# Graph network on one core: seven lookup units in the second tile, twelve in the fourth, masks between evictions

## The reference

```
adj_d = adjacency with own nodes, some neighbours dropped by rank
vals  = where(adj_d > 0, x[neighbour, channel], inf)
s     = sort(vals, over neighbours)
agg   = sum over tau in (0.25, 0.5, 0.75) of w[tau] *
        (s[lo] + frac * (s[hi] - s[lo]))      # per node and channel
out   = relu((x + agg) @ W1 + b1) @ W2 + b2
```

## Time and profile before

| | us |
|---|---|
| median of 3 runs | 3977.04 (3974.77 to 3978.62) |
| profiled execution | 3979.06 |
| its span, first to last instruction | 3976.9 |
| DVE busy | 3539.2 |
| PE busy | 2607.1 |
| ACT busy | 1764.2 |

### The profile page before, as it was taken

How to read it: one execution, slowest core, us unless ns; L and a number is a source line. 1 busy time by engine, 2 the same in 40 slices (tenths; PEclk the granted TensorE clock), 3 DMA queues, 4 the chain that set the end, 5 groups by cost and what they waited for, 6 DMA issues and landing times. The chain is left out here.

```text
span 3976.9 us, 44051 instructions
## 1 busy us (share of the span) xinstructions
PE 2607.1 (66%) x14922; PEld 1083.3 (27%) x14922; DVE 3539.2 (89%) x6052; ACT 1764.2 (44%) x2295; POOL 56.6 (1%) x47
## 2 busy tenths in 40 slices
PE   0000042868686777777777878687868686877897
PEld 0000021223222232323222322232323222223665
DVE  7999989999989999899999998999998999964676
ACT  2112341646464545455554545463636364643232
POOL 0005000000000000000000000000000000000000
PEclk6555565979797989888988888898989898978777
DMA  1010000323232323232323222232323231322011
GB/s 24 0 32 11 0 6 18 44 41 65 35 56 36 59 32 58 32 58 34 56 35 54 38 50 41 46 46 43 49 40 50 38 66 28 54 46 41 33 42 32
DMA packets 242541, 156.06 MB, mean 39 GB/s; under 512 B 126472, under 2 KB 227994, under 8 KB 242330
## 3 DMA queue, kind: packets, MB, share of 16 engines
q1 hardware_dynamic: 238202, 152.36, 22.2%
q10 hardware_dynamic: 4128, 1.05, 0.2%
HBM read 39.07 MB, written 13.63 MB: 13 GB/s over the span
## 5 line engine op out<-in xcount | busy, mean ns | idle before, releaser
L901 ACT ACTIVATE hot<-bcast,eq_bias 128x1024 bf16<-128x1024 f32 x744 | 826.7, 1111 | 575.1 <-PE bcast L559 574.0
L1216 DVE SCALAR_TENSOR_TENSOR prod<-near,iota_b,rows 128x512 f32<-128x512 bf16 x768 | 571.9, 745 | 209.3 <-PE rows L571 107.1
L571 PE MATMUL rows<-hot,table 128*64 128x512 bf16 x4608 | 699.3, 411 | 68.0 <-DVE prod L1216 62.1
L547 PE MATMUL ring<-member,neigh_t 128*128 128x512 bf16 x2048 | 571.2, 419 | 183.2 <-ACT words L875 72.4
L558 PE MATMUL bcast<-idx_t,sel_a 128*128 128x512 f16 x744 | 304.5, 409 | 207.4 <-ACT hot L901 195.3
L580 PE MATMUL found_bank<-prod,sum_to 128*64 128x512 f32 x1536 | 432.6, 628 | 4.4 <-DVE prod L1216 4.4
L1276 DVE TENSOR_TENSOR picked<-picked 128x6144 uint16<-128x6144 uint16 (+2 forms) x192 | 387.5, 2018 | 0.7
L571 PEld LDWEIGHTS rows<-hot,table 128*64 128x64 bf16 x4608 | 222.0, 113 | 512.2 <-issue 401.6
L547 PEld LDWEIGHTS ring<-member,neigh_t 128*128 128x128 bf16 x2048 | 183.7, 105 | 599.6 <-issue 238.8
L474 PE MATMUL ring<-ident,swapped 128*128 128x128 f32 x32 | 6.2, 355 | 504.1 <-DVEq L1072 503.9
L559 PE MATMUL bcast<-idx_t,sel_a 128*128 128x512 f16 x744 | 303.6, 408 | 0.0
(11 more groups left out here) (325 smaller groups left out, 4245.6 us busy)
## 6 DMA issues: line engine op xcount, KB each, us to landing
near<-idx_bt SPq DMA_DIRECT2D x768, 128.0 KB
late<-in_adj_dram SPq DMA_DIRECT2D x16, 1024.0 KB, 5.3
adjt_d<-late SPq DMA_DIRECT2D x16, 512.0 KB, 2.7
adj_l<-adjt_d SPq DMA_DIRECT2D x16, 512.0 KB, 5.8
adj_s<-adjt_d SPq DMA_DIRECT2D x16, 512.0 KB, 3.6
parts_d<-parts SPq DMA_DIRECT2D x6, 512.0 KB, 5.1
table<-parts_d SPq DMA_DIRECT2D x192, 16.0 KB, 2.2
out_dram<-x_all SPq DMA_DIRECT2D x4, 512.0 KB, 3.8
```

The source lines that it names most:

```text
L547: ins = mm(ring[u % 2][:, :], kept_t[:, j, P * i:P * i + P], member[:, j, n // 2, 512 * (n % 2):512 * (n % 2) + 512], start=(j == 0), stop ...
L571: ins = mm(rows[u % 2][C * h:C * h + C, :], table[:, s, 2 * g8 + h, :], hot[:, u % HOT, h, :], start=(s == 0), stop=(s == 2))
L901: run(hot[:, u % HOT].rearrange(flat), spread_bank(l, u)[0][:, 0:2, :].rearrange(flat), ACT.Relu, bias=eq_bias[:, :]).then_inc(S["hot_read ...
L1216: stt(out=prod[:, u % DEEP, :], in0=near[:, u % NEAR, :], scalar=iota_b[:, :], in1=rows[u % 2][:, :], op0=ALU.is_equal, op1=ALU.mult).then ...
```

## The change

`PLACES` gives tile 1 seven units instead of nine (none behind its steps 1 and 2) and tile 3 twelve instead of ten (two behind step 4 and two behind step 6). `LEAD` goes from 0, 4, 13, 23, 33 to 0, 4, 11, 21, 33. PE and ACT used to work out how far ahead they run from the number of units of the tile; now a list `AHEAD` says it, and a `min` keeps them from running into the units of the tile behind too early. On ACT the masks of tile 1 stand one ahead of the eviction of chunk (1,6), one behind it, and one behind chunk (1,7). The copy to `x_now` moves from the middle of tile 0 to the end of `select`.

```diff
-PLACES = ((6, 7, 8, 9), (1, 2, 3, 4, 5, 6, 7, 8, 9), tuple(range(10)), tuple(range(10)))
+PLACES = ((6, 7, 8, 9), (3, 4, 5, 6, 7, 8, 9), tuple(range(10)), (0, 1, 2, 3, 4, 4, 5, 6, 6, 7, 8, 9))
+AHEAD = (0, -1, 1, 3)
@@ PE, select @@
-                        units(l, LEAD[i] + s + len(PLACES[i]) - 9)
+                        units(l, min(LEAD[i] + AHEAD[i] + s, LEAD[i + 1]))
@@ ACT, select @@
                 units(l, 4)
-                if l is not None:
-                    run(x_now[:, :, :], xb(l), ACT.Copy).then_inc(S["x_copied"], 1)
                 chunk(b, 1, 4)
                 units(l, 5)
                 chunk(b, 1, 5)
                 units(l, 6)
-                for k in range(TAUS):
-                    mask(b, 1, k)
+                mask(b, 1, 0)
                 chunk(b, 1, 6)
+                mask(b, 1, 1)
                 chunk(b, 1, 7)
+                mask(b, 1, 2)
                 for i in range(1, NT):
-                    level = LEAD[i] + len(PLACES[i]) - 9 + 2
+                    level = LEAD[i] + AHEAD[i] + 2
                     for s in range(10):
                         if i + 1 < NT:
                             if s == 2:
                                 mask(b, i + 1, 0)
-                                units(l, level + 2)
+                                units(l, min(level + 2, LEAD[i + 1] + 2))
                                 mask(b, i + 1, 1)
-                                units(l, level + 3)
+                                units(l, min(level + 3, LEAD[i + 1] + 2))
                                 mask(b, i + 1, 2)
                             if s < CW:
                                 chunk(b, i + 1, s)
-                        units(l, level + s)
+                        units(l, min(level + s, LEAD[i + 1] + 2))
+                if l is not None:
+                    run(x_now[:, :, :], xb(l), ACT.Copy).then_inc(S["x_copied"], 1)
```

## The result

The changed kernel takes 3919.99 us (median of 4 runs, 3918.85 to 3921.05) against 3976.95 us (4 runs, 3974.77 to 3978.62): a ratio of 0.9857, 95% interval 0.984 to 0.9874, that is 57 us or 1.4% faster. The forecast was 3908 with a range of 3885 to 3945.

What follows compares the result with a forecast made beforehand. DVE sets the pace, so only its idle time can be won: three tiles fall from 81.5 us by 4.8 a round, 67 us over 14 rounds plus 3 for round 1, together 70, giving 3908 us, range 3885 to 3945.

Steps and rivals of the forecast that it cites:

- The bound: DVE, busy 89% of the span, sets the pace; two rows of lookup waits hold 187.6 us; busy time stays near 3539.
- Tile 1: Second tile of a round: falls from 30.2 to 23.7 us, no wait before its first unit, 0.75 at its third.
- Tile 2: Third tile of a round: its wait stays and grows 0.3 us, so 27.2 us for 26.85.
- the one on the clock: PE's slow clock in five rounds of tile 1 goes with the shorter stand; if it stays, 8 us come back (3916).
- Tile 3: Last tile, two more units: 25.8 us for 24.5 with no wait; at most 3.3 us of waits a round.
- rival C: Tile 3, with twelve units, becomes PE's: at 2.6 us a unit 31.2 us, kernel 3988; loop expected about 2.0; chance 0.05.
- The last part of the round: The stretch behind the tiles: no term in the sum, so length as before.
- signs of being wrong: Tile 1 keeps over 2 us of waits, tile 3 gets over 1, or the round's last part gets longer.
- A: Tile 1's stall moves instead of going: DVE stands 3.5 us at unit 6, gain 1.8 a round, 3953; chance 0.14.
- B: PE gets ahead in tile 2 too, its 2.35 us of wait go: 3885 for half, 3861 for all; chance 0.08.
- D: No effect: the moved units cost in tile 3 what tile 1 gains, a loop near 2.5, 3977; chance 0.04.
- The queue of SP: SP's hold in tile 3 ends 0.66 us later, but unit 33 comes 1.3 later too: costs nothing.

Runs made afterwards that it cites:

- experiment 1: Kernel before, with only tile 1's masks placed one by one around the evictions of chunks (1,6) and (1,7): 3955.59 us, ratio 0.9949.
- experiment 2: Changed kernel with tile 1's three masks in a row again, ahead of both evictions, so the moved units without the mask change: 3935.50 us, ratio 0.9907.
- Experiment 6: Changed kernel plus eight matmuls whose output nothing reads, on PE just ahead of chunk (3,4) in tile 2: 3917.35 us, ratio 0.9847.
- Experiment 5: Kernel of experiment 4 with four more units moved from tile 2 (six left) to tile 3 (sixteen): 3923.76 us, ratio 0.9862.
- Experiment 7: Kernel of experiment 4 with PE issuing unit 39 ahead of the second count and the dense product in the last part: 3844.85 us, ratio 0.9662.
- experiment 3: Changed kernel with the copy to `x_now` put back in the middle of tile 0: 3917.92 us, ratio 0.9854.
- experiment 4: Changed kernel with ACT evicting chunk (i+1,2) behind the second mask instead of the third in tiles 1 and 2: 3873.39 us, ratio 0.9745.

## Why the prediction was right, and where it was off

**The bound.** The two rows of DVE's waits fell by 54.9 us of the 60.2 that the span lost. DVE's busy time, which I had forecast unchanged, fell from 3539.2 to 3533.4, though it runs the same 6052 instructions; no run says why.

**Tile 1.** Forecast 23.7 with no wait before its first unit and 0.75 before its third; measured 23.72 with 0.74 in seven of the thirteen rounds, 23.35 in one, and 22.88 with none in five. In the round at 1439.7, one of the five, PE starts chunk (2,0) 0.6 us ahead of DVE's tile, in the one at 2190.8 it is 0.3 behind it; I had worked out only the second kind. The average is 23.37, a gain of 6.9 where I had 6.5. The steps behind it held too: PE's stand before chunk (2,0) is 0.69 for the forecast 0.7; ACT evicts (2,2) 8.93 us into the tile (2222.10) for the forecast 9.05, and PE's chunk (2,4) follows 0.64 later for 0.6. Experiments 1 and 2 show that each part of the change gives a share of the gain.

**Tile 2.** Forecast 27.2, measured 27.15 in nine rounds. The step that failed is the one on the clock. I took the slow rounds as gone with the 2.66 us stand, and set them only against tile 1. They went there, but the 2.13 us stand of tile 2 now has them in four rounds: 1.6 x 4 = 6 us. The prediction had the sentence for it (8 us come back if it stays), and the price was right and the place wrong. Experiment 6 ties it to the stand. All four rounds are among the five with no wait in tile 1, so what tile 1 gave beyond the forecast and what tile 2 lost come in the same rounds: together the two tiles take 51.6 us there and 50.0 to 50.9 in the others. That tile 1 came out better than forecast was luck, and it hides 4 of the 6 us.

**Tile 3.** Forecast 25.8, measured 25.78 with no wait in any round. Experiment 5 bears out the reasoning: with a lookup every 2.0 us, the figure set against rival C, twelve units fit and sixteen don't.

**The last part of the round.** Forecast as before; measured 0.80 us longer a round, 0.80 x 13 = 10 us. The prediction named a longer last part among its signs of being wrong, and on this term it was: the sum has nothing for it. This is the larger part of the 10 to 13 us by which I overrated the gain. I had taken its length as one number, though the kernel before had two kinds of rounds, 86 to 88 us and over 88, depending on where TensorE's clock fell. In its two long rounds the dense product ahead of unit 39's lookup ran at low clock already (1.97 us) and DVE waited 2.27 for that lookup; in ten the product took 1.10 to 1.25 and DVE waited 0.38 to 1.01; in one the clock stayed up there and DVE didn't wait. In the changed kernel ten rounds are of the first kind (waits of 1.37 to 2.27) and three of the last (waits of 0.20 at most). Experiment 7 shows that place and removes the wait; experiment 3 takes the copy off the list. Why the slow case is met in ten rounds instead of two isn't settled. That the clock falls and rises at other places once a round has another length fits all tables, but no run fixed those places and varied nothing else.

**The rivals.** A would have left 3.5 us of wait at unit 6, which isn't there. B did not come about on its own, since tile 2 kept its wait, but experiment 4 shows that its 2.8 us were to be had by one moved line. C exists and lies past twelve units. D would have shown as waits in tile 3. The queue of SP cost nothing: no new wait for a transfer stands in the tiles.

**The clock.** In tile 2 the granted clock is 0.94 in the four slow rounds, and 1.00 in all rounds of experiment 6, where PE is kept busy. The Trainium skill, "TensorE: Matmul & The Clock Gate", Part 1, says that activity releases the throttle. Experiment 6 agrees. The runs add that a stand of 2.13 us was followed by the fall in four rounds and not in nine. One reading of the prediction was off: it has the 2.66 us stand in nine rounds with no fall, and it was eight. In the ninth, the round at 882.1, PE stood 1.23 us before chunk (2,0), and the clock fell in that tile (0.94), behind a stand of 1.90; the chunk took 1.78 us for 1.04:

```profile
916.78 1.78 PE L547 MATMUL ring<-member,neigh_t 128*128 128x512 bf16 x4 [1.90 <-ACT words L875]
```

## What to carry to other kernels

Where engines work through fixed lists, follow a wait back to the list in which something ready stands behind something that nobody wants yet; such moves (experiments 1, 4 and 7) gave 20 to 47 us each here without saving any work, and their size can be worked out from starts in the time line to a few tenths of a microsecond. Take work that fills gaps out of the stretch where the feeding engines are behind, and put it where they stand, but set the loop that feeds it against the demand before packing it denser. And when a stage has two lengths in the trace, forecast both and how often, not the one that was looked at.

## What the runs showed of the hardware that was not expected

Stands of PE of the same length were followed by either level of the clock. In the kernel before, the stand of 2.66 us was followed by full clock in eight rounds and by 1.2 GHz in five, and the one of 1.90 by 1.2 GHz in two (tile 2 of round 1, tile 1 of round 2) and by full clock in the others; in tile 2 of the changed kernel the stand of 2.13 was followed by full clock in nine rounds and by 1.2 GHz in four. In tiles 1 and 2 each fall cost DVE 1.6 us. Where DVE wanted nothing from PE a fall cost nothing: in experiment 7 the granted clock was 0.50 from 2094.0 to 2096.2 and DVE was busy throughout. The table load of ACT took 1.28 us, and one was enough for the nine masks of a round, even with evictions and `hot` instructions between the masks.
